# Sixteen-head windowed attention in a six-layer stack: score products over 64 rows with halves moved by DMA, values used where they are copied, and a new order of all engines

## What is computed

```python
def attn_layer(x, Wqkv, qs, ksc, Wo):          # x: (4, 512, 128); 16 heads of 64
    q, k, v = split(x @ Wqkv)                  # into heads
    q, k = l2norm(q) * qs, l2norm(k) * ksc
    q = q * cos * scale + rotate_half(q) * sin * scale
    k = k * cos / scale + rotate_half(k) * sin / scale
    # windows of 32: query window w sees key windows w-1 and w
    sim = 8.0 * einsum('bhwie,bhwje->bhwij', q, look(k)); sim[mask] = -inf
    return einsum('bhwij,bhwje->bhwie', softmax(sim), look(v)) @ Wo
def ffn_layer(x, ...):                         # layernorm, 341 wide, gated by gelu
for i in range(6):
    x = attn_layer(shift_tokens(x), ...) + x
    x = ffn_layer(shift_tokens(x), ...) + x
```

## Time and profile before

| what | before |
|---|---|
| median of 3 runs | 2498.02 us (2496.93 to 2498.21) |
| profiled execution: its time, its span | 2506.73 us, 2504.8 us |
| mean granted clock of PE | 0.966 |
| busy in the span: PE, DVE, ACT, POOL | 2354.9, 1717.0, 1597.2, 1451.3 us |
| moved by DMA | 204.60 MB |

### The profile page before, as it was taken

The page is one execution under the profiler, slowest core; times in us unless marked ns, Lnnn a source line. Parts: engine busy times, 40 slices in busy tenths (PEclk is TensorE's granted clock), DMA queues, the critical chain, the costliest instruction groups (busy, mean ns, idle before and its releaser), DMA issues.

```text
span 2504.8 us, 121652 instructions
## 1 busy us (share of the span) xinstructions
PE 2354.9 (94%) x53677; PEld 1748.5 (70%) x53677; DVE 1717.0 (69%) x3393; ACT 1597.2 (64%) x5036; POOL 1451.3 (58%) x1408
## 2 busy tenths in 40 slices
PE   9958999999999999999999999999888999999967
PEld 8836777777777777677777777777645666666657
DVE  4477788777888888787788788887335555555534
ACT  3226777777777787777777778777625454545422
POOL 1166667656676676566666677665117656656307
PEclk9969999999999999999999999999979999999978
DMA  4013333433333334333343333333216222222136
GB/s 91 15 33 86 79 83 94 97 80 83 91 93 95 82 83 103 83 92 87 80 96 90 80 92 87 87 87 87 54 30 177 49 48 48 48 48 48 31 97 249
DMA packets 230208, 204.60 MB, mean 82 GB/s; under 512 B 133687, under 2 KB 155464, under 8 KB 229552
## 3 DMA queue, kind: packets, MB, share of 16 engines
q1 hardware_dynamic: 225296, 190.91, 30.5%
q0 software_dynamic: 2208, 5.58, 0.7%
q10 hardware_dynamic: 2176, 0.33, 0.1%
HBM read 86.05 MB, written 15.70 MB: 41 GB/s over the span
## 4 chain that ended last, share of the span: by engine, by line
PE 66%; DVE 12%; SPq 6%; ACT 5%; issue 5%; POOL 4%; DMA 3%; POOLq 0%; ACTq 0%; DVEq 0%
PE psum L1211 7%; PE psum L1959 5%; PE psum L1237 5%; PE psum L1229 5%; PE psum L1938 4%; PE psum L1111 4%; PE psum L1944 3%; PE psum L1113 3%; PE psum L1112 3%; PE psum L1993 3%; PE psum L1983 3%; ACT p L1357 3%; SPq L972 3%; PE psum L1188 2%; PE psum L1219 2%
## 5 line engine op out<-in xcount | busy, mean ns | idle before, releaser
L1357 ACT ACTIVATE p<-p,stat 128x64 f32<-128x64 f32 x1536 | 512.4, 336 | 47.2 <-DVE stat L1491 44.9
L1577 POOL TENSOR_TENSOR p<-p,inverse 128x512 f32<-128x512 f32 x192 | 200.2, 1043 | 456.5 <-DVE inverse L1494 452.2
L1211 PE MATMUL psum<-kT,qT 32*32 32x64 f32 x24576 | 305.5, 224 | 25.8 <-issue 24.2
L2092 DVE TENSOR_REDUCE largest<-psum 128x1 f32<-128x512 f32 x256 | 165.0, 687 | 228.0 <-PE psum L1944 228.0
L1211 PEld LDWEIGHTS psum<-kT,qT 32*32 32x32 f32 x24576 | 264.1, 103 | 75.3 <-issue 74.3
L1357 ACT ACTIVATION_READ_ACCUMULATOR p<-p,stat 128x1 f32 x1536 | 288.6, 188 | 0.0
L1421 DVE SCALAR_TENSOR_TENSOR rotated<-psum,scales,rotary 128x512 f32<-128x512 f32 x384 | 270.8, 742 | 25.8 <-ACT sq L1293 25.8
L1556 POOL TENSOR_TENSOR squares<-sq 128x512 f32<-128x512 f32 x192 | 245.3, 1278 | 44.3 <-ACT sq L1293 43.8
L1293 ACT ACTIVATE sq<-psum 128x512 f32<-128x512 f32 x384 | 213.7, 582 | 57.3 <-PE psum L1113 54.6
L1229 PEld LDWEIGHTS psum<-pT,v_win 64*64 64x64 f32 x12288 | 198.6, 136 | 64.7 <-issue 45.9
L1111 PE MATMUL psum<-xs,wqkv_high 128*128 128x512 f32 x384 | 205.7, 536 | 23.2 <-DVE rotated L1421 22.9
(11 more groups left out here) (351 smaller groups left out, 5402.3 us busy)
## 6 DMA issues: line engine op xcount, KB each, us to landing
v_win<-v_tok SPq DMA_DIRECT2D x576, 128.0 KB
rnorm_wide<-rnorms SPq DMA_DIRECT2D x384, 64.0 KB
v_win<-v_tok SPq DMA_DIRECT2D x336, 64.0 KB
q_rows<-q_rows_all SPq DMA_DIRECT2D x32, 512.0 KB, 4.6
tile_weights<-expert_table SPq DMA_DIRECT2D x23, 512.0 KB, 5.8
wqkv<-L_ffn_Wqkv SPq DMA_DIRECT2D x96, 64.0 KB, 2.2
rel_values<-sq SPq DMA_DIRECT2D x60, 64.0 KB, 2.2
wo<-L_ffn_Wo SPq DMA_DIRECT2D x48, 64.0 KB
```

Source lines behind the costliest of these rows:

```text
L1211: last = PE.e.matmul(psum[WIN * blk:WIN * (blk + 1), f, out], q[rows, g, half, tok:tok + WIN], k[rows, g, half, tok:tok + 2 * WIN], start= ...
L1357: last = A.e.activation(p, p, ACT.Exp, bias=t.stat[:, h, 2 * g + f:2 * g + f + 1], accum_out=t.sum[:, h, g, f:f + 1])
L1577: G.e.tensor_tensor(p, p, t.inv[:, h, :, :].unsqueeze(3).to_broadcast([P, GROUPS_TF, 2, 2 * WIN]), ALU.mult).then_inc(*t.p_scaled.by(m))
L2092: V.e.tensor_reduce(t.mx[n % 4][:, :], psum[:, n % 5, :], AX, ALU.max, negate=True).then_inc(*t.largest.by(n))
```

## The change

The order constants: a unit has 128 steps instead of 32, a part 16 instead of 4, and nearly every step gets a place of its own. Beside that:

- **Scores** over whole heads. POOL writes rotated queries to one of six stages (`t.stage`), DVE writes the scaled keys to stages too (two instructions of 128 x 512 a group instead of one in place of 128 x 1024), and SP moves each stage by two DMAs of 64 partitions (`relay`), so that the two halves of a head lie in the same tile on neighbouring partitions. A head then takes one product over 64 rows: 32 products a part instead of 64. The score step waits for all relays of the unit.
- **Bank of a score**: `swapped(f, blk)`, f for the blocks 0 and 1, 1 - f for 2 and 3.
- **Values** are copied to `v_win` itself (`[:, 0, ...]`), where blocks 1 and 3 use them as they are; blocks 0 and 2 use a second copy `[:, 1, ...]`, moved by six DMAs (four in a unit's first tile). For f = 1 the tokens of the value products are taken from `x_swapped`, in which POOL has exchanged the 64-token halves of each tile (four copies a unit).
- **Norms**: `norms_wide` is one DMA of 256 KB whose source has 4 x 32 x 512 elements; the root has scratch of its own; ACT copies the query norms by three instructions instead of one.
- **Projections** start after the high part of the shift and wait for the low one before their third matmul. Squares are added in place, in three buffers. `pT` has one buffer instead of two.

```diff
-UNITS_TF, UNIT, TILE, PART = DEPTH * B, 32, 8, 4
+UNITS_TF, UNIT, TILE, PART, PIECE = DEPTH * B, 128, 32, 16, 16
-PART_FIRST = 39
-PART_AT = {"score": 0, "keep": 0, "largest": 1, "exp": 2, "inverse": 3, "scale": 3, "turn": 5, "turn_copy": 6, "weigh": 6, "o_copy": 8, "mix": 9, "add": 9}
+PART_FIRST = 156
+PART_AT = {"score": 0, "keep": 0, "largest": 4, "exp": 9, "inverse": 12, "scale": 12, "turn": 20, "turn_copy": 24, "weigh": 24,
+           "o_copy": 28, "mix": 39, "add": 44}
-VALUE_FIRST, WINDOWS_AT = 29, 31
+VALUE_FIRST, VALUE_AT, VALUE_COPY_AT = 132, (0, 8), (3, 15)
+WINDOWS_AT = (142, 174, 206, 241)
+RELAY_LAG, K_RELAY_LAG = (16, 16, 18, 16), (3, 6, -1, 2)
-SPREAD_AT = (16, 18, 19, 24)
-SCALE_AT = (24, 28, 29, 32)
+SPREAD_AT = (77, 80, 104, 116)
+SCALE_AT = (99, 112, 124, 132)
...
 def norms_wide(c, t, u, g):
...
-    for j in range(4):
-        src = bass.AP(t.rn_dram[u % 2].tensor, (j * GROUPS_TF + g) * S, [[0, HALF_D], [1, S]])
-        SP.e.dma_start(t.wide[g % 2][HALF_D * j:HALF_D * (j + 1), :], src).then_inc(*t.wide_in[g % 2].by((u, g, j)))
+    src = bass.AP(t.rn_dram[u % 2].tensor, g * S, [[GROUPS_TF * S, 4], [0, HALF_D], [1, S]])
+    SP.e.dma_start(t.wide[x % WIDES][:, :], src).then_inc(*t.wide_in[x % WIDES].by(x))
+def relay(c, t, u, kind, g):
+    SP = c.SP
+    if u >= 2:
+        SP.wait_ge(*t.scored.on((u - 1) * PARTS - 1))
+    for half in range(2):
+        k = stage_of(u, kind, g, half)
+        for e in range(2):
+            to = t.q[u % 2][half::2, g, e, :] if kind else t.k[u % 2][half::2, g, e, WIN:WIN + S]
+            SP.e.dma_start(to, t.stage[k % STAGES][e * H64:(e + 1) * H64, :]).then_inc(*t.relayed[k % STAGES].by((k, e)))
...
+    SP.e.dma_start(v[WIN:P, 1, 0, :, :], v[0:P - WIN, 0, 0, :, :]).then_inc(*v_in.by((n, 0)))
+    SP.e.dma_start(v[w1, 1, 1, :, :], v[w0, 0, 1, :, :]).then_inc(*v_in.by((n, 1)))
+    SP.e.dma_start(v[w0, 1, 1, :, :], v[w3, 0, 1, :, :]).then_inc(*v_in.by((n, 2)))
+    SP.e.dma_start(v[w3, 1, 1, :, :], v[w2, 0, 1, :, :]).then_inc(*v_in.by((n, 3)))
+    if n % TPB:
+        SP.e.dma_start(v[w0, 1, 0, :, :], before[w3, 0, 0, :, :]).then_inc(*v_in.by((n, 4)))
+        SP.e.dma_start(v[w2, 1, 1, :, :], before[w1, 0, 1, :, :]).then_inc(*v_in.by((n, 5)))
...
 def part_tensor(c, t, m, s):
     if s == PART_AT["score"]:
-        PE.wait_ge(*t.k_scaled.on((u, GROUPS_TF - 1)))
-        PE.wait_ge(*t.made.on((u, 2 * GROUPS_TF - 1)))
+        for back in range(STAGES):
+            PE.wait_ge(*relayed_on(t, 4 * GROUPS_TF * (u + 1) - 1 - back))
...
         for g in range(GROUPS_TF):
-            for half in range(2):
-                for blk in range(TPB):
-                    tok, out = i * P + blk * WIN, slice(g * 2 * WIN, (g + 1) * 2 * WIN)
-                    for f in range(2):
-                        j = 2 * h + f
-                        rows = slice(HALF_D * j, HALF_D * (j + 1))
-                        last = PE.e.matmul(psum[WIN * blk:WIN * (blk + 1), f, out], q[rows, g, half, tok:tok + WIN], k[rows, g, half, tok:tok + 2 * WIN],
-                                           start=False, stop=(half == 1 and g == GROUPS_TF - 1))
+            for blk in range(TPB):
+                tok, out = i * P + blk * WIN, slice(g * 2 * WIN, (g + 1) * 2 * WIN)
+                for f in range(2):
+                    rows = slice(DH * f, DH * (f + 1))
+                    last = PE.e.matmul(psum[WIN * blk:WIN * (blk + 1), swapped(f, blk), out], q[rows, g, h, tok:tok + WIN], k[rows, g, h, tok:tok + 2 * WIN],
+                                       start=False, stop=(g == GROUPS_TF - 1))
...
-        V.e.tensor_tensor(k, k, t.wide[g % 2][:, :].unsqueeze(1).to_broadcast([P, 2, S]), ALU.mult).then_inc(*t.k_scaled.by((u, g)))
+            for half in range(2):
+                k = stage_of(u, 0, g, half)
+                if k >= STAGES:
+                    V.wait_ge(*relayed_on(t, k - STAGES))
+                last = V.e.tensor_tensor(t.stage[k % STAGES][:, :], t.k[u % 2][:, g, half, WIN:WIN + S], t.wide[x % WIDES][:, :], ALU.mult)
+            last.then_inc(*t.k_scaled.by((u, g)))
...
+    if s == SWAP_AT:
+        if u:
+            G.wait_ge(*t.valued.on((u * TPB - 1, 1)))
+        for k in range(2):
+            for to, x in swap_halves(t, u, k):
+                last = G.e.tensor_copy(to, x)
+        last.then_inc(*t.swapped.by(u))
```

More of the change, by code:

```diff
@@ L790, in transformer_setup @@
     t.xs = [[sb(f"xs{i}_{k}", [P, S], F32R) for k in range(2)] for i in range(2)]
-    t.xf = sb("x_ffn", [P, S])
+    t.xp = [sb(f"x_swapped{k}", [P, S], F32R) for k in range(2)]
+    t.xf = c.sq4[2]
     t.q = [sb(f"qT{i}", [P, GROUPS_TF, 2, S]) for i in range(2)]
@@ L1401, in transformer_vector, with rotate @@
                 unit_vector(c, t, n, s)
+def rotate(c, t, u, p, half):
+    V, psum, (l, b), (kind, g, lo) = c.V, c.psum, divmod(u, B), piece(p)
+    cos, sin = (t.tab[:, 2 * (1 - kind) + x, :] for x in range(2))
+    V.wait_ge(*t.squared.on((u, (p, half))))
+    if u or p:
+        V.wait_ge(*t.made.on((u, p - 1) if p else (u - 1, 2 * GROUPS_TF - 1)))
+    if u >= 2:
+        V.wait_ge(*t.scored.on((u - 1) * PARTS - 1))
+    if kind:
+        for k in (stage_of(u, kind, g, x) for x in range(2)):
+            if k >= STAGES:
+                V.wait_ge(*relayed_on(t, k - STAGES))
+    first, second = made_of(t, u, kind, g)
+    if half == 0:
+        outs = ((first, cos), (t.turned_by[1][:, :], sin))
+    else:
+        outs = ((t.turned_by[0][:, :], sin), (second, cos))
+    for out, table in outs:
+        last = V.e.scalar_tensor_tensor(out=out, in0=psum[:, 4 + half, :], scalar=t.scales[:, kind, half, l:l + 1], in1=table, op0=ALU.mult, op1=ALU.mult)
+    last.then_inc(*t.rotated.by((u, (p, half))))
```

262 lines of the change are left out of this document (143 added, 119 removed).

## The result

The changed kernel took 2560.06 us (median of 4 runs, 2555.89 to 2562.81) where the kernel before, on the same chip, took 2497.47: a ratio of 1.0257, 95% interval 1.0239 to 1.0276. The forecast was 2383 us and faster. The profiled execution took 2555.89 us with a span of 2554.0 us, and PE's mean clock fell from 0.966 to 0.949.

The account below looks back on a forecast made before the run. PE was taken to set the 68.04 us period. Scores 5.6 plus issue idling 0.5 minus 1.1 gave 5.0 us a period, 115 us over 23 periods: 2383 us, own range 2345 to 2420, overall 2330 to 2475.

Parts of the forecast that it names:

- What bounds the kernel now: Transformer: PE sets the 68.04 us period; DVE has 12.7 us of room a unit, ACT 15.7.
- Scores: PE's score products: 64 records a part at 10.9 ns, 0.70 us instead of 1.40, saving 5.6 us a unit.
- Rival A: Score tiles cost like 64 x 64, 16.6 ns a record; 2.7 us saved a unit, 2436 us; chance 0.12.
- Given back: PE's waits other than issue, 1.15 us a unit, grow to 2.1 as DVE's room shrinks: +1.0 us.
- Idling unchanged: Lower end of the main case's own range: PE's idling does not grow, 6.1 us a period saved, 140 in all.
- DVE: Key scaling in eight halves instead of four costs +0.2 us a unit; DVE at 55.5 of 62.4 us, 89%.
- SP, DMAs, relays: 58 issues a unit, some 35 us, DMA engines near 0.5; hidden, with 6.2 us of cover for the last relay.
- POOL's swap: POOL's four copies of 128 x 256 cost 2.5 us a unit (5.1 at most), hidden at step 112.
- ACT +0.6: ACT's small extra copies of query norms and one x_ffn column add 0.6 us a unit: 52.9 of 62.4 us.
- C: Relays behind SP's wait make scores late; PE idles and turns cold, 2.5 us a unit more, 2556 us; chance 0.09.
- E: All is given back: a part's chain is paced by ACT or DVE at 68 us; no change, chance 0.03.
- B: DVE's keys come late behind the norms' DMA on few engines; 3.0 of 5.0 us lost, 2452 us; chance 0.11.

Follow-up runs that it names:

- e14: Kernel before with one Newton step instead of three in the transformer's roots, 5.2 us of DVE work less a unit: 2480.51 us, ratio 0.9951.
- e1: Kernel before in its own order, score products halved to 32 over 64 rows a part, operands not whole heads, nothing relayed: 2459.25 us, ratio 0.9849.
- e2: Kernel before with the changed kernel's order of steps, on the old data flow with long scores and no relays: 2606.25 us, ratio 1.0445.
- e9: Kernel before with the new order and halved score products on operands that are not whole heads, old data flow: 2523.04 us, ratio 1.0106.
- e10: Changed kernel with the queries' root at step 133 instead of 148 and their transpose at 149 instead of 155: 2611.33 us, ratio 1.0482.
- e11: Changed kernel with the next unit's shift at step -16 instead of -8 on ACT and POOL: 2597.14 us, ratio 1.0412.
- e12: Changed kernel with both the queries' root and transpose and the next unit's shift moved earlier: 2591.91 us, ratio 1.0392.
- e13: Changed kernel with one Newton step instead of three in the transformer's roots, 5.2 us of DVE work less a unit: 2489.44 us, ratio 0.9993.
- e17: Changed kernel with a part's maxima on DVE taken over the own window's 32 keys only, 256 of 512 columns: 2552.33 us, ratio 1.019.
- e18: Changed kernel with one Newton step instead of three for the keys' norms alone (root at step 68): 2540.66 us, ratio 1.0124.
- e6: Changed kernel without any relay DMA and without the waits for them, so scores read other data: 2545.2 us, ratio 1.018.
- e7: Changed kernel with POOL's four copies to x_swapped replaced by a one-column memset: 2558.86 us, ratio 1.0251.
- e15: Changed kernel with ACT's copy of pT made twice, one behind the other, in every part: 2574.87 us, ratio 1.034.
- e3: Changed kernel with the one 256 KB norms broadcast a group split into four DMAs of 64 KB, as before: 2613.79 us, ratio 1.0463.
- e8: Changed kernel with each score product issued twice, giving PE about the score time of before: 2683.64 us, ratio 1.0749.
- e16: Changed kernel with POOL scaling only half of p, 256 of 512 columns: 2549.46 us, ratio 1.0236.
- e5: Changed kernel's data flow in nearly the old order, most steps at four times their old round: 2669.64 us, ratio 1.0688.

## Why the prediction was wrong, point by point

**What bounds the kernel now: right, and over-read.** PE did set the pace (e14: a tenth for DVE's work). But "what is taken from PE is gained until one of them, or a wait, takes over" used busy shares for the room of the others. DVE's 12.7 us of room a unit are no stock that is used up last. One run shows it without any of the new order: e1 took 115 us from PE and gained 38, and PE stood waiting for steps of a part's chain while DVE was busy 85% of the stretch. That the room lies in pieces between its duties to each part is my reading of it.

**Scores: right in kind, mis-sized by an eighth.** 0.79 us a part and not 0.70, 12.3 ns a record; 4.9 us a unit in place of 5.6, 16 us in all. Rival A is refuted: both groups of rows change their banks, and not at L1229's 16.6 ns; e1, where each group keeps its bank, has the same 0.79 us. The Trainium skill's "TensorEngine Tiling (Array Packing)", Gotcha 1, says that different row tiles cannot access the same PSUM bank at once. The changed kernel does not test that: but for the changes between blocks, two products that follow one another write different banks, so the rule speaks against this change less than the prediction had it.

**The failing step is "Given back", with the order taken as neutral.** The prediction scaled today's 1.15 us of waits by DVE's room and came to +1.0 us a unit; "the finer order could make it 0". The runs measured +4.6 us of idling and +2.7 of slower work, most of it by the colder clock: 7.4 us a unit. The square separates two parts of it:
- In the order before, the short scores alone raise idling by 2.9 us a unit (e1). The scaling by room was too small by a factor of three.
- The new order adds 111 us to the kernel before and 64 to e1 (e2, e9). "PE's colder clock after a longer gap is in this" took the clock to follow the idling: with short scores the new order adds 0.5 us of idling a unit and 2.5 us of slower work. The prediction read from the constants only the distances of relays, norms and windows, where it found cover. It did not put the old and new distances side by side. Root to transpose went from 24 steps to 7, low shift to projection from 16 to 8. The first could be costed from the rows of before: nine steps of 0.33 us, 638 and 432 ns, 4.0 us of root in 7 x 0.49 = 3.4 us, late by 0.6 before any queueing. It then came 1.6 us late, since the integer steps took 0.8 and 1.2 us.

That the distances explain the 64 to 111 us is not shown: giving them back, one by one and both, cost 34 to 56 us (e10, e11, e12). Why the same amount of idling leaves the clock at 1.00 in the one order and at 0.95 in the other stays open.

**The range.** "Idling unchanged" gives 2498 - 140 = 2358 us and not the 2345 at which the range began; the error has no part in the miss, which is on the other side.

**DVE: +0.2 us forecast, +3.1 measured** (1791.7 - 1717.0, over 24). The scaling by halves is 1.4 of it, L219 of 128 x 128 1.6 and its 128 x 4 form 1.0; some other rows fell. All three are operations that stand beside POOL's. DVE's time would have been nearly harmless before (e14) and is not now: at the shares of e13, e17 and e18, a third to seven tenths, these 75 us would be worth 25 to 52 (an estimate). Only half of the 75 comes with the new flow: e9, with the new order and the old flow, has DVE busy for 1753.5 us, with L219 at 1214 ns. The other 38 us would be worth 13 to 27 of the new flow's 38 us of time, and 19 are gone when the relays are (e6). How the 38 divide exactly stays open.

**SP, DMAs, relays: right on PE, with a price left out.** The cover held (0.5 us of PE's waits in 20 units), queue 1 moved 241.25 MB, the DMA share went to 0.45 to 0.49, "near 0.5". Relays cost 19 us with all that hangs on them, a term that the prediction had at nothing. The waits that they make are DVE's, for a free stage (L1535 in the table above, 90.2 us), which it did not price.

**POOL's swap: right** (e7). **ACT +0.6**: it came to +0.9 (1619.4 - 1597.2, over 24), and ACT's time is cheap (e15).

**Rivals.** C is the only one on the right side, and its 2556 us are within 4 us of the result. That is luck. It is still refuted: its mechanism (relays late behind SP's wait, PE idle for over 3.3 us in one gap) did not occur; no gap of PE's exceeded 2.5 us in the stretch. Its chain "gap, then cold clock" is right in kind. E's idea, that a part's chain paces at ACT or DVE, comes nearest, though not with one engine: DVE and PE by turns, and ACT hardly. B's late norms did not show: no wait of DVE's for them stands in the changed kernel's trace, where 13.3 us stood before, and the cure cost 51 us (e3).

**What the runs support as the cause.** Shown by the square: +111 us for the order, -85 for the short scores in it, +38 for the new flow. What lies behind it is in part argued. In the kernel before, one engine was full, and the other engines' times hid behind it: DVE 10%. Once PE is no longer full, PE's work counts at 80% (e8) and DVE's at 30 to 70% (e13, e17, e18), the copy on ACT at about a fifth (e15), the scaling on POOL at less than that (e16: 5 of 80 us, not clear of noise). The shares of PE and DVE add up to about one or more. I read that as the two standing in line, PE making what DVE keeps and DVE what PE turns, with order and clock between them. The changed kernel added to DVE and shortened the distances between it and PE, and its PE ran at a colder clock.

**The best version run** is e1's arrangement, 2459 us, with operands that don't make the attention's scores; it marks what short scores are worth if the halves could be put together at no cost in the old order. The one that does put them together in nearly that order is e5, 2670 us. No kernel that computes all of the reference beat the kernel before.

## What to carry to other kernels

When the full engine gets less to do, don't divide the others' idle time by the new period: take the distance in steps between each producer and its consumer in the new order, turn it into time at the new pace, and hold the producer's measured duration against it, above all where an order is rewritten. Measure each engine's worth by giving it a known amount of work more or less, since the longest wait in the list can be a symptom: here curing it cost 2%. Look at PE's busy time and granted clock beside its idle time, since an order can cost through them with the same idling. A reordering and a new data flow should be timed apart, in a square of four kernels, before they are judged together.
